# Two banks for the turned probabilities, one for the values of all heads, and a later place for the output parts in each head

## The reference, cut to what matters

```python
scores = jnp.einsum('bhtd,bhsd->bhts', q, k) / scale      # 16 heads, 256 x 256 each
attn = jax.nn.softmax(scores, axis=-1)
out = jnp.einsum('bhts,bhsd->bhtd', attn, v)              # values
return out.transpose(...).reshape(...) @ Wo               # projection

h = jax.nn.silu(bitlinear158(x, w1, b1))                  # 256 -> 1024
h = jax.nn.gelu(h, approximate=False)
h = layer_norm(h, ln_g, ln_b)
return bitlinear158(h, w2, b2)                            # 1024 -> 256
```

## Time and profile before

| | |
|---|---|
| time, median of three runs | 547.52 us |
| time of the profiled execution | 546.43 us |
| its span in the trace | 544.5 us |
| attention loop in the trace | about 262 to 513 us |
| PE busy over the span | 485.3 us (89%) |
| DVE busy | 436.0 us (80%) |
| ACT busy | 393.5 us (72%) |
| POOL busy | 246.4 us (45%) |

### The profile page before, as it was taken

How to read it: one execution, slowest core, us unless ns; L and a number is a source line. 1 busy time by engine, 2 the same in 40 slices (tenths; PEclk the granted TensorE clock), 3 DMA queues, 4 the chain that set the end, 5 groups by cost and what they waited for, 6 DMA issues and landing times.

```text
span 544.5 us, 10844 instructions
## 1 busy us (share of the span) xinstructions
PE 485.3 (89%) x3402; PEld 399.9 (73%) x3402; DVE 436.0 (80%) x1213; ACT 393.5 (72%) x928; POOL 246.4 (45%) x255
## 2 busy tenths in 40 slices
PE   8958888799997999998999999987999889997925
PEld 6445555666787677777899999976999789986804
DVE  4889999999968487986668559869888699766887
ACT  2786777585374567886877777898687997798654
POOL 1139999894106656302772376125861232122121
PEclk9958999899999999998999999999899999999867
DMA  6655887572788997925220034001660000000000
GB/s 178 152 173 176 230 272 225 173 220 78 206 256 244 291 316 213 301 92 194 59 69 2 17 77 59 7 2 17 77 82 3 2 1 1 22 1 0 2 20 19
DMA packets 52558, 61.65 MB, mean 113 GB/s; under 512 B 6284, under 2 KB 42742, under 8 KB 52502
## 3 DMA queue, kind: packets, MB, share of 16 engines
q1 hardware_dynamic: 48662, 49.43, 30.5%
q0 software_dynamic: 3840, 11.54, 10.0%
HBM read 54.27 MB, written 6.69 MB: 112 GB/s over the span
## 4 chain that ended last, share of the span: by engine, by line
PE 49%; issue 17%; DVE 14%; ACT 12%; POOL 6%; DMA 2%; DVEq 0%; SPq 0%; ACTq 0%; POOLq 0%
PE ps L1712 8%; PE ps L1650 7%; PE ps L1651 6%; PE ps L1652 6%; DVE hst L1968 4%; PE ps L1701 4%; PE ps L1568 3%; PE ps L1370 2%; ACT pr L1085 2%; POOL dbu L636 2%; DVE hc L1980 2%; PE ps L1604 2%; PE ps L1589 2%; POOL G L683 1%; PE ps L1378 1%
## 5 line engine op out<-in xcount | busy, mean ns | idle before, releaser
L636 POOL TENSOR_TENSOR dbu<-du,brow 128x512 f32<-128x512 f32 x64 | 82.4, 1324 | 22.3 <-DVE du L1955 18.7
L721 POOL TENSOR_TENSOR pn<-pr,pinv 128x256 f32<-128x256 f32 x64 | 40.9, 639 | 107.8 <-DVE pinv L2376 107.3
L1712 PE MATMUL ps<-pT,cS 128*128 128x256 f32 x256 | 67.4, 386 | 0.0
L1085 ACT ACTIVATE pr<-ebuf,smin 128x256 f32<-128x256 f32 x128 | 63.6, 501 | 2.4 <-issue 1.8
L872 ACT ACTIVATE ps<-dtv,amat 128x510 f32<-128x510 f32 x64 | 44.0, 695 | 24.4 <-DVE hst L1968 19.5
L683 POOL DMA_INDIRECT G<-token_rows,idx_x x32 | 37.8, 1180 | 43.1 <-DVE wkv L2104 20.8
L705 POOL DMA_INDIRECT G<-expert_out,idx_g x48 | 50.9, 1061 | 11.5 <-issue 11.1
L2366 DVE CUSTOM_DVE_ANT_0 ebuf<-ps,mbias 128x256 f32<-128x256 f32 x128 | 49.0, 420 | 2.6 <-issue 2.6
L1650 PE MATMUL ps<-xnT,mqk 128*128 128x256 f32 x128 | 47.2, 368 | 4.3 <-DVE qT L2336 2.5
L1701 PE MATMUL ps<-ident,pn 128*128 128x128 f32 x256 | 39.5, 277 | 9.2 <-ACT pT L1100 5.0
L1712 PEld LDWEIGHTS ps<-pT,cS 128*128 128x128 f32 x256 | 44.8, 193 | 3.9
(11 more groups left out here) (387 smaller groups left out, 1486.2 us busy)
## 6 DMA issues: line engine op xcount, KB each, us to landing
brow<-state_rows SPq DMA_DIRECT2D x16, 512.0 KB, 4.0
wdn<-in_L_ffn_wd SPq DMA_DIRECT2D x12, 384.0 KB, 6.7
ebuf<-state_rows SPq DMA_DIRECT2D x17, 256.0 KB, 5.4
wgu<-in_L_ffn_wg SPq DMA_DIRECT2D x11, 384.0 KB, 5.3
wgu<-in_L_ffn_wu SPq DMA_DIRECT2D x11, 384.0 KB, 7.3
expert_out<-xn SPq DMA_DIRECT2D x11, 256.0 KB, 4.3
wo<-in_L_xattn_Wo SPq DMA_DIRECT2D x4, 512.0 KB, 5.8
wq<-in_L_xattn_Wq SPq DMA_DIRECT2D x4, 512.0 KB, 5.7
```

Source lines behind the costliest of these rows:

```text
L636: nc.gpsimd.tensor_tensor(dbu[:, j, :], du[:, j % 2, at:at + 512], brow[:, pair % BRING, j // 2, :], ALU.mult).then_inc(pool_dbu, 1)
L1085: last = A(pr[:, h % 2, tt, :], sneg[:, h % 2, tt, :], ACT.Exp, scale=-1.0, bias=smin[:, h % 2, tt:tt + 1], accum_out=psum_[:, h % 2, tt:t ...
L1712: last = pe.matmul(ps[:, 3 + 2 * (h % 2), 0:L], cS[:, b % 2, st, :], pT[:, h % 2, st, :], start=(st == 0), stop=(st == 1))
```

## The change

The transposed probabilities of even and odd heads go to banks 4 and 5, and `turn_p` waits for the copy of the head before last and no longer for that of the last head. The values of all heads go to bank 3, even heads to its first half and odd heads to its second; `values` waits for `o_low` of the last head and no longer of the head before last. Within a slot, `values` moves behind `queries` and `project` on PE, `o_high` moves behind `normal_half` and `exps` on ACT, and `o_low` moves behind `q_low` on DVE.

```diff
+        def values_out(h):
+            return ps[:, 3, L * (h % 2):L * (h % 2) + L]
...
-                A(pT[:, h % 2].rearrange("p a b -> p (a b)"), bank(4), ACT.Copy).then_inc(pT_ready, 1)
+                A(pT[:, h % 2].rearrange("p a b -> p (a b)"), bank(4 + h % 2), ACT.Copy).then_inc(pT_ready, 1)
...
-                A(oT[0][:, h % 2], bank(3 + 2 * (h % 2))[:, 0:L], ACT.Copy).then_inc(o_hi, 1)
+                A(oT[0][:, h % 2], values_out(h), ACT.Copy).then_inc(o_hi, 1)
...
-                if 4 <= slot < NH * B + 4:
-                    o_high((slot - 4) // NH, (slot - 4) % NH)
                 if slot + 2 < NH * B:
                     q_high((slot + 2) // NH, (slot + 2) % NH)
...
                 if slot < NH * B:
                     exps(b, h)
+                if 4 <= slot < NH * B + 4:
+                    o_high((slot - 4) // NH, (slot - 4) % NH)
...
-                wait_count(pe, pT_ready, i)
+                wait_count(pe, pT_ready, i - 1)
...
-                        last = pe.transpose(ps[:, 4, L * st + P * tt:L * st + P * tt + P],
+                        last = pe.transpose(ps[:, 4 + h % 2, L * st + P * tt:L * st + P * tt + P],
...
-                wait_count(pe, o_ready, i - 1)
+                wait_count(pe, o_ready, i)
                 for st in range(2):
-                    last = pe.matmul(ps[:, 3 + 2 * (h % 2), 0:L], cS[:, b % 2, st, :], pT[:, h % 2, st, :], start=(st == 0),
+                    last = pe.matmul(values_out(h), cS[:, b % 2, st, :], pT[:, h % 2, st, :], start=(st == 0),
...
-                if 4 <= slot < NH * B + 4:
-                    values((slot - 4) // NH, (slot - 4) % NH)
                 if slot + 2 < NH * B:
                     queries((slot + 2) // NH, (slot + 2) % NH)
                 if 5 <= slot < NH * B + 5:
                     project((slot - 5) // NH, (slot - 5) % NH)
+                if 4 <= slot < NH * B + 4:
+                    values((slot - 4) // NH, (slot - 4) % NH)
...
-                low(oT[1][:, h % 2], bank(3 + 2 * (h % 2))[:, 0:L], oT[0][:, h % 2], o_ready)
+                low(oT[1][:, h % 2], values_out(h), oT[0][:, h % 2], o_ready)
...
+                if slot + 2 < NH * B:
+                    q_low((slot + 2) // NH, (slot + 2) % NH)
                 if 4 <= slot < NH * B + 4:
                     o_low((slot - 4) // NH, (slot - 4) % NH)
-                if slot + 2 < NH * B:
-                    q_low((slot + 2) // NH, (slot + 2) % NH)
```

## The result

The changed kernel takes 566.45 us, the median of four runs (565.93 to 567.61), beside 547.49 for the kernel before on the same chip: a ratio of 1.0356, with an interval of 1.0329 to 1.0384. It is slower, as forecast, but by 19.0 us and not by the 9.9 of the sum, and outside the range. The profiled execution took 566.75 us (span 565.0).

The account below looks back on a forecast made before the run. PE was taken as full in ordinary slots and held in three stretches by a chain leaving ACT, which is behind. Terms 3.2 + 3.8 + 2.7 + 0.15 = 9.9 us on 546.43 gave 556.3, as median 557; range 549 to 562.

Parts of the forecast that it names:

- third stretch and drain: Feed-forward part f = 2 and the loop's last slots: the moves cost +2.7 us, bounds +0.6 and +4.2.
- Part 1, the second bank at nothing: turn_p no longer waits for the last copy, but waits on POOL and q_low remain: 0, bounds 0 and -5.0 us.
- Part 2, the one values bank at nothing: values waits for the o_low that project, directly before it, waits for anyway: nothing either way.
- Ordinary slots at nothing: Slots of 3.43 us: o_low ends 1.1 us into the next, project starts at 2.04, so the delay is covered.
- the batch's start: Start of batch 1, placed at slot 13 without feed-forward: norm_high stands behind o_high, +0.15 us.
- First stretch, +3.2: Feed-forward f = 0, about 358 to 383 us: a later variance, passed by POOL to PE; bounds +2.0 and +4.9.
- (b): Slot 31: ACT stands still 0.74 us, since middle, giving the first deviations their mean, comes behind o_low.
- (c): variance starts 3.26 us after the second deviations start, not 1.28, behind normal_half, exps, o_high and o_low: +2.0 us.
- Second stretch, +3.8: Feed-forward f = 1, about 425 to 447 us: +3.2 up to the root, then later values and scaling; bounds +2.3, +5.5.
- Third stretch, +0.6: f = 2, until project in slot 64: inverse behind o_low and second deviations behind o_high, about +0.6 us.
- rival C: Worse: project, behind exps and ACT's table load in slots 31 and 47, waits over 2 us, lowering the clock: 560, chance 0.2.
- Drain, +2.1: From slot 65 nothing hides project, values and both copies, 2.55 us in series: four slots, some 0.5 us each.

Follow-up runs that it names:

- warm: The whole change plus unread transposes keeping PE busy in the long waits of slots 46 and 61: 566.71 us, 1.0395 against the kernel before.
- hidden_behind: The whole change with ACT's turned_hidden of batch 2 in slot 67 moved behind o_high: 564.48 us, 1.0325 against the kernel before.
- the two halves: Two runs against the kernel before: only the bank and wait changes, 549.14 us; only the three moves with the old banks, 565.73 us.
- the banks alone: The kernel before with the change's banks and waits and none of its moves: 549.14 us, 1.003.
- values_early: The whole change with values put ahead of queries and project on PE again: 607.99 us, 1.1097 against the kernel before.
- banks_gathers: The kernel before with the change's banks, the old orders, and POOL's gathers one head later in one batch: 548.55 us, 1.0014.
- old_in_stretches: The whole change with the three moves taken back in slots 28 to 39, 44 to 55 and from 58: 550.04 us, 1.0063 against before.
- orders_alone: The kernel before with the three moves and its old banks: 565.73 us, 1.0352.
- drain_old: The whole change with the three moves taken back from slot 64 on: 564.48 us, 1.0313 against the kernel before.
- queries_first: The whole change with values between queries and project, and o_high ahead of normal_half again: 549.9 us, 1.0039 against the kernel before.

## Why the prediction was wrong, point by point

The direction was right, and so was the mechanism of the first two stretches. The step that failed is **third stretch and drain**, "Sum +2.7", which measured 8.3. The runs show three things there that it left out or made too small: the low clock, worth 2.7 us by `warm`; ACT's `turned_hidden` ahead of `o_high` in slot 67, worth 1.6 us from slot 64 on in `hidden_behind` beside `warm`; and from slot 56 to 64, with the clock's share taken off, 1.8 us where 0.6 was forecast. With the series of copies, 2.2 us where 2.1 was forecast, that is 2.7 + 1.6 + 1.8 + 2.2 = 8.3. Each of these rests on one execution. The other misses are smaller.

- *Part 1, the second bank at nothing:* right in time, by the two halves. The reason given, that the waits on POOL and `q_low` remain, holds for the change only in part: with the banks alone the gain is lost before POOL's wait. By the Trainium skill, page Perfetto Trace Analysis, section Optimization Strategy, a repeated gap on the full engine can mean that a buffer is missing. Here the gap had the name of a buffer, the buffer was given, and nothing was gained: 549.14 beside 547.38 us.
- *Part 2, the one values bank at nothing:* right for the change (1.0356 with both banks, 1.0352 without), where `project` waits for the same `o_low` directly before. With `values` ahead it isn't nothing: `values_early`, and in the old order the waits of `banks_gathers`.
- *Ordinary slots at nothing:* right for most: 3.40 us a slot, and `old_in_stretches`. Of the 1.02 us of slots 3 to 28, 0.35 are the batch's start in slot 14 (forecast 0.15); 0.5 in slot 25, with as much in slots 41 and 57, and 0.2 in slot 21 were not foreseen, and no run took them apart.
- *First stretch, +3.2:* right, 3.62. (b) shows as ACT's wait for the mean, (c) as 3.25 us where 3.26 was forecast. The `project` of slot 31 waits 2.09 us; the prediction named it as a sign but gave it no price, since the later wait for POOL hides it. In slots 35 to 44 it left out that `add_attention`, with which DVE frees the projection's bank, is queued behind `o_low` as well: 0.85 us of PE in slot 37 and as much behind the second stretch. The rest of the 1.02 us there is a balance: slots 36 and 37 lost 0.86 and 1.13 in all, other slots 0.26, and slot 35 took 1.24 less, since no low clock followed its wait (1.00 in 385 to 390, where before had 0.67 in 380 to 385).
- *Second stretch, +3.8:* 5.49 with what follows it. Up to slot 51 it is 4.13, near the forecast; the rest is from slot 51 to 56, most of it in slot 53 with the wait of 0.85 us behind `add_attention`. The clock (0.69 in 435 to 440) has no part in it, since `orders_alone` lost 5.53 at full clock.
- *Third stretch, +0.6:* 3.82. The prediction followed `inverse` and the deviations there and gave `project` behind `exps` and the table load to rival C, for slots 31 and 47. It happened in slot 61: 2.10 us, and then the clock at 0.52. `warm` puts the clock there at 2.7 us from slot 61 to the last projection, about 2.0 of it up to slot 64. Without it, 1.8 us are left: 1.1 up to slot 61 and 0.73 behind it.
- *Drain, +2.1:* 4.48. The series of copies was priced about right, a PE wait of 0.49 us in slot 65, for instance; missing were 1.85 us at the last projection, where `turned_hidden` stood ahead of `o_high` on ACT (1.4 of it by `hidden_behind`), and the low clock in slot 64. With `turned_hidden` moved and the clock at 1.00 there, `hidden_behind` loses 2.20 us in this part, near the forecast.
- *Rival C* was nearer than the sum: it had `project` behind `exps` and ACT's table load, and the low clock in the drain. Its price (3.2 us over the forecast) was too small, the low clock of the second stretch cost nothing, and of its two slots 31 has the long wait (2.09 us, no low clock) and 47 only 0.91 us.

What stays open: why the clock fell in different places in executions of the same code, and which of the two edits of `queries_first` gives back more.

## What to carry to other kernels

When a step is moved behind others in an in-order list, look up everything that is queued behind its consumer on the next engine, at every place of the program where one of the engines has no lead, the drain above all, and not only on the chain that ends last now; here moves that are nearly free in 30 slots cost some 16 us in the rest. A second buffer gained nothing here, where the engine that empties it was behind; check that before counting the waits that carry its name. Before a low clock gets a price, look whether the engine was the slow one there: the same half speed cost nothing in one slot and 1.6 us four slots on. And look for what stands in front on the engine that the last wait names: moving POOL's gathers by a head in one batch gave 2.4 us, with nothing changed in the work.

## What was not expected of the hardware

Waits of PE of about the same length don't always bring the low clock: the 2.09 us before 370.00 were followed by 1.00 from 370 to 380, and at the 2.10 before 506.06 the clock went to 0.52 in 505 to 510. And the place differs between executions of the same instructions (0.69 in 435 to 440 after; 1.00 there and 0.66 in 445 to 450 in `drain_old`). The table load on ACT in front of `exps` took 1.28 us, and the next instruction started 1.30 after its start:

```profile
502.89 1.28 ACT L1088 ACT_TABLE_LOAD   x1
504.19 0.51 ACT L1088 ACTIVATE pr<-ebuf,smin 128x256 f32<-128x256 f32 x1
```
